# A graph-and-experts kernel on one core: order of TensorE's queue in the first gate, constant products in front of waits, and two starts of loops

## The reference, cut to what matters

```python
x = x + gnn0(layernorm(x), adj)      # U = eigenvectors of the normalised Laplacian (64 x 64);
                                     # U ( relu((U^T x) W1 + b1) W2 + b2 )
x = x + ffn0(layernorm(x))           # 8 experts, top 2 of (x Wg + bg), softmax of the two logits as weights:
                                     # sum_e w_e (gelu(x W1[e] + b1[e]) W2[e] + b2[e]),  hidden size 512
x = x + gnn1(layernorm(x), adj)      # h = relu(adj (x Wg0 + bg0)); h = relu(adj (h Wg1 + bg1));
                                     # then for p = 1..4 an LSTM over windows of p tokens, whose last
                                     # hidden state replaces the last token of its window
x = x + ffn1(layernorm(x))           # H = gelu(x W1 + b1); probs = softmax(H Wg + bg); the expert e of the
                                     # largest prob: prob * (H Wd[e] + bd[e])
```

## Time and profile before

| | |
|---|---|
| time, median of 3 runs | 1427.07 us (1426.35 to 1429.05) |
| the profiled execution's own time | 1429.24 us |
| its span | 1427.5 us |
| TensorE, busy share of the span | 78% (1110.5 us) |
| VectorE | 57% (813.1 us) |
| ScalarE | 52% (747.9 us) |
| GpSimd | 38% (537.7 us) |
| mean granted clock of TensorE | 0.902 |

### The profile page before, as it was taken

The page is one execution under the profiler, slowest core; times in us unless marked ns, Lnnn a source line. Parts: engine busy times, 40 slices in busy tenths (PEclk is TensorE's granted clock), DMA queues, the critical chain, the costliest instruction groups (busy, mean ns, idle before and its releaser), DMA issues. The chain is left out here.

```text
span 1427.5 us, 27849 instructions
## 1 busy us (share of the span) xinstructions
PE 1110.5 (78%) x6302; PEld 823.2 (58%) x6303; DVE 813.1 (57%) x3799; ACT 747.9 (52%) x2079; POOL 537.7 (38%) x837
## 2 busy tenths in 40 slices
PE   3444424568744999999949999999999689929995
PEld 2223313456644999999936663445444245529995
DVE  7777798958772433354558973444444478622221
ACT  4555555515322666666626765655555366415552
POOL 5666513302577770255447500000000005645554
PEclk9999965879757999999969999999999799959998
DMA  9500000000112332333311100000000002243330
GB/s 260 144 1 1 1 1 1 1 4 16 36 64 85 118 120 66 89 103 104 102 46 50 40 1 0 0 1 0 0 1 0 4 6 85 90 130 110 106 103 27
DMA packets 85701, 75.57 MB, mean 53 GB/s; under 512 B 13207, under 2 KB 74848, under 8 KB 85613
## 3 DMA queue, kind: packets, MB, share of 16 engines
q1 hardware_dynamic: 71788, 44.64, 11.3%
q0 software_dynamic: 13824, 29.98, 6.7%
HBM read 41.72 MB, written 33.37 MB: 53 GB/s over the span
## 5 line engine op out<-in xcount | busy, mean ns | idle before, releaser
L1249 POOL DMA_INDIRECT z<-spent,seats x64 | 63.3, 990 | 393.5 <-DVE spent L1370 376.1
L1716 ACT ACTIVATE c_H<-ps,c_b 128x128 f32<-128x128 f32 x576 | 156.9, 383 | 99.5 <-PE ps L1762 99.5
L2278 PE MATMUL ps<-BIG,spent 128*128 x364 | 156.1, 578 | 3.3 <-ACTq L2291 3.3
L1762 PE MATMUL ps<-ZS,c_w 128*128 128x128 f32 x1152 | 142.5, 277 | 2.9 <-ACT ZS L1705 1.7
L1748 PE MATMUL ps<-spent,c_H 128*128 x1152 | 140.3, 275 | 0.0
L1762 PEld LDWEIGHTS ps<-ZS,c_w 128*128 128x128 f32 x1152 | 136.0, 194 | 3.9 <-ACT ZS L1705 2.4
L1748 PEld LDWEIGHTS ps<-spent,c_H 128*128 128x128 f32 x1152 | 134.3, 192 | 0.0
L2278 PEld LDWEIGHTS ps<-BIG,spent 128*128 128x128 f32 x364 | 69.7, 192 | 84.7 <-issue 84.7
L2286 PE MATMUL ps<-e_hs,spent 128*128 128x512 f32 (+1 forms) x256 | 110.0, 572 | 0.0
L897 POOL DMA_INDIRECT z<-BIG,spots x64 | 63.5, 993 | 111.1 <-DVE spots L1014 93.7
L1616 POOL DMA_INDIRECT c_rows<-y,seats x64 | 60.6, 946 | 113.9 <-DMA y<-c_ys 60.0
(11 more groups left out here) (534 smaller groups left out, 2599.2 us busy)
## 6 DMA issues: line engine op xcount, KB each, us to landing
BIG<-z SPq DMA_DIRECT2D x72, 129.0 KB, 2.1
ZB<-z SPq DMA_DIRECT2D x144, 64.0 KB
y<-c_ys SPq DMA_DIRECT2D x72, 128.0 KB
spent<-in_L_ffn_W_dram SPq DMA_DIRECT2D x1, 2048.0 KB
spent<-in_L_ffn_W_dram SPq DMA_DIRECT2D x8, 256.0 KB
w_dn<-in_L_ffn_Wd_dram SPq DMA_DIRECT2D x8, 256.0 KB
z<-BIG,spots POOLq DMA_INDIRECT x128, 2.2
z<-j_padding SPq DMA_DIRECT2D x9, 129.0 KB, 2.6
```

The lines of the kernel that those rows point to most:

```text
L1249: pool.indirect_dma_start(z, bass.IndirectOffsetOnAxis(ap=k.seats[:, 0, n:n + 1], axis=0), k.R[:, row(n), :], None, bounds_check=E * STRID ...
L1716: act.activation(H[u][:, c, h * P:(h + 1) * P], UP[u][c // 2][:, o:o + P], ACT.Gelu, bias=b1[u][h][:, c:c + 1]).then_inc(gelu, 1)
L1762: pe.matmul(UP[u][c // 2][:, o:o + P], w1[u][h][:, c * P:(c + 1) * P], ZT[u][:, h * P:(h + 1) * P], start=True, stop=True).then_inc(up, 1)
L2278: last = pe.matmul(view(k.ps[4 * u + j], wide, lanes), k.w_ihT[:, w, :], state(i, u, s, p, wide, lanes), start=True, stop=(s == 0))
```

## The change

There is a new helper. It issues products of constant bf16 values into a PSUM bank that is free at that place; nothing reads the result.

```diff
 # gate0, VectorE
-            if LAG + 2 <= g <= GROUPS + LAG + 1:
+            if g % 2 and 0 <= g - LAG - 2 < GROUPS:
                 add_gate_bias(g - LAG - 2)
...
             if 2 <= g <= GROUPS + 1:
                 stats(g - 2)
+            if g % 2 and 0 <= g - LAG - 1 < GROUPS:
+                add_gate_bias(g - LAG - 1)
 # gate0, TensorE (mix(g) holds the mixing products that stood at the loop's head)
+        mix(0)
         for g in range(GROUPS + LAG + 4):
...
-            if ranks:
-                rank((g - 11) // 2)
...
-                if ranks:
-                    pe.wait_ge(rank_read, (g - 11) // 2 + 1)
+                if g >= 12:
+                    pe.wait_ge(rank_read, (g - 10) // 2)
...
                 last.then_inc(turned, 1)
+            if g + 1 < GROUPS:
+                mix(g + 1)
+            if ranks:
+                rank((g - 11) // 2)
 # first experts, TensorE (second experts alike)
-            if not known or t < NT - 1:
+            if not known or 0 < t < NT - 1:
                 turn(t + 1, 1 - u, r + u, first)
...
+        pe.wait_ge(k.gate0_scattered, 16 * (TILES - 2))
+        keep_busy(pe, Y[1], k.ones16, 14)
         turn(0, 0, 0, 0)
+        turn(1, 1, 0, 0)
 # gate1, TensorE
+        keep_busy(pe, UP[3], k.ones16, 4)
         for g in range(3):
             lift(g)
+            keep_busy(pe, UP[3], k.ones16, 4 if g < 2 else 12)
...
     def ahead(g):
-        return range(3, LIFTED + 1) if g == 0 else range(g + LIFTED, min(g + LIFTED + 1, GROUPS))
+        return (range(3, 4), range(4, LIFTED + 2))[g] if g < 2 else range(g + LIFTED, min(g + LIFTED + 1, GROUPS))
 # gnn1, VectorE
+            hidden(0)
             for j in range(GT):
                 combine(2 * GT + j)
                 stats(2 * GT + j)
+            add_bias(0)
             for g in range(GROUPS + 2):
-                if 1 <= g <= GROUPS:
+                if 2 <= g <= GROUPS:
                     add_bias(g - 1)
```

More of the change, by code:

```diff
@@ L452, in _ @@
             token_rows(GROUPS - 1)
+            keep_busy(pe, ps[7], both, 5)
             pe.wait_ge(s_vectors, 1)
@@ L455, in _ @@
             pe.wait_ge(s_zw_sb, GROUPS)
+            keep_busy(pe, ps[7], both, 2)
             pe.wait_ge(s_sides, 1)
@@ L464, in _ @@
             pe.matmul(ps[2][0:N, 0:N], U[:, :], LU[:, :], start=True, stop=True).then_inc(s_forms, 1)
+            keep_busy(pe, ps[7], both, 2)
             pe.wait_ge(s_ritz, 1)
             pe.matmul(ps[4][0:N, 0:N], ones[0:N, 0:N], offd[:, :], start=True, stop=True).then_inc(s_ritz_row, 1)
+            keep_busy(pe, ps[7], both, 8)
             pe.wait_ge(s_factor, 1)
@@ L469, in _ @@
             pe.matmul(ps[0][:, 0:N], E2[:, :], UT2[:, 0:N], start=True, stop=True).then_inc(s_refined, 1)
+            keep_busy(pe, ps[7], both, 3)
         @block.vector
@@ L1139, in rank, with mix @@
             pe.matmul(RANK, k.upper16[:, :], marks, start=False, stop=True).then_inc(ranked, 1)
+        def mix(g):
+            if g >= 2:
+                pe.wait_ge(h_ready, g - 1)
+            for j in range(GT):
+                c = slice(j * P, (j + 1) * P)
+                last = pe.matmul(MIX[g % 2][:, c], k.BIG[:, g * GC + j * P:g * GC + (j + 1) * P], k.BDU[:, :],
+                                 start=True, stop=True)
+            last.then_inc(mixed, 1)
+        mix(0)
         for g in range(GROUPS + LAG + 4):
             u = g % 2
[L1143 to L1150, removed]
             if 2 <= g <= GROUPS + 1:
@@ L1402, in gate_vector @@
                 root_of(1, nothing())
-                back(4)
-                back(5)
             elif g % 2 and g + 3 < GROUPS:
+                if g == 1:
+                    back(4)
+                    back(5)
+                    link.need(link.n)
                 spread((g + 3) // 2, beside)
@@ L1529, in gate_tensor @@
             for n in ahead(g):
+                if g == 0:
+                    keep_busy(pe, SC, k.ones16, 4)
                 lift(n)
@@ L1717, in step @@
                                    bias=b1[u][h][:, c:c + 1]).then_inc(gelu, 1)
-            if not (isinstance(t, int) and t == NT - 1):
+            if not (isinstance(t, int) and t in (0, NT - 1)):
                 turn_out(t + 1, 1 - u)
         turn_out(0, 0)
+        turn_out(1, 1)
         for t in range(2):
@@ L1843, in experts_sync @@
         for b in range(RING):
-            sp.wait_ge(k.scattered[b], 16 * PAIR * len(range(b, GROUPS // 2, RING)))
+            sp.wait_ge(k.scattered[b], 16 * sum(n < TILES - 2 for n in range(TILES) if n // PAIR % RING == b))
+        sp.wait_ge(k.last_scattered, 16 * 2)
         def fetch(t, b, r):
@@ L1928, in step @@
             if isinstance(t, int) and t == 0:
+                last = (GROUPS // 2 - 1) % RING
+                pe.wait_ge(k.scattered[last], 16 * (PAIR * len(range(last, GROUPS // 2, RING)) - 2))
+                keep_busy(pe, Y[1], k.ones16, 14)
                 turn(0, 0, 0)
+                turn(1, 1, 0)
             pe.wait_ge(turned_sb, t + 1)
@@ L2192, in _ @@
             pe.matmul(GATE[1][:, 0:D], floor[:, 0:P], k.w_g1[:, 1, :], start=True, stop=True).then_inc(outer, 1)
+            pe.wait_ge(used, GT)
+            keep_busy(pe, GATE[2], k.ones16, 12)
             for g in range(GROUPS + 1):
```

17 lines of the change are left out of this document (11 added, 6 removed).

## The result

The changed kernel takes 1417.12 us (median of 4 runs, 1417.02 to 1419.32), the kernel before 1426.71 in the same comparison (4 runs, 1425.09 to 1429.05): a ratio of 0.9931 with a 95% interval of 0.9919 to 0.9942, some 9.6 us less. The sign is as forecast; the time lies 1.1 us outside the range, and 9.6 of the 22 us came. The two profiled executions took 1429.24 and 1417.02 us, 12.2 apart: that of before lies 2.5 above its median, so 2.6 us of what the two profiles show as gain is not in the medians.

A forecast was written before the change was run, and what follows sets the result against it. TensorE was taken to bound the last stage, VectorE's waits for TensorE the first gate. 2.5 + 10 + 1.9 + 3.8 + 3.0 + 1.0 = 22.2 us turned the 1427.07 median into 1405, range 1400 to 1416 (forecast's own 1400 to 1408).

The forecast's parts named there:

- Price of a product: One constant bf16 product of 512 columns was estimated at 0.43 us at 1.2 GHz and 0.21 us at 2.4.
- End of the spectrum, 2.5: 20 products in waits before the first gate raise the clock for its start: gain 2.5 us, 0 if not risen by 300.
- Ranks last, 10: First gate: the new order removes VectorE's 10.9 us of waits for TensorE, leaving 0.9; gain 10 us (3 to 11).
- 8.7 us a pair: TensorE's work per pair in the first gate's loop at the high clock level, against VectorE's 10.5 us.
- First and second experts, 1.9 and 1.0: Fillers before turn 0, turn 1 before up 0: gains 1.9 us (first experts) and 1.0 us (second, or loss up to 1.0).
- up 0 ... takes 1.8 us instead of 3.6: First experts: up-projection 0 begins later, at 447.1 instead of about 445.6, but takes half as long.
- about 4.8 us before the first turn: First experts: when the 14 products start after scatter 62 landed, so they end 0.2 to 1.0 us late.
- the rival in which the level is lost between fillers and work: Both experts' starts gain nothing (0 and +1.0), the second gate 1.7 us; sum 17.0, time 1410 us; chance 16%.
- Second gate, 3.0: Fillers between lifts speed up 0 to 3.6 us from 5.51; lifts 4 and 5 move behind up 1; gain 3.0 us.
- Second graph stage, 3.8: Hidden 0 and bias 0 move ahead on VectorE, so bias 1 comes at 757.0 instead of 760.80; gain 3.8 us.
- the rival in which the products do no good: Products never raise the level in time: first gate gains 9, graph stage 2.9, others lose 0.6; 1416 us; chance 11%.
- the three signs of being wrong: VectorE's waits reappear under the moved gate bias; level drops in the loop; turn 1's load costs up 0 more than gained.

The follow-up runs named there:

- loop_fill: turn_behind plus 8 constant products in front of the gating products in the first gate's even iterations 8 to 18; 1411.47 us, ratio 0.9892 to the kernel before.
- loop_only: The kernel before with only the first gate's reordering (mixing ahead, ranks last, both gate biases in odd iterations), no constant products; 1420.99 us, ratio 0.9962.
- rank_first: turn_behind with the ranks in front of the next mixing instead of behind it in the first gate's odd iterations; 1409.49 us, ratio 0.9878 to the kernel before.
- pe_order: The kernel before with only TensorE's new order in the first gate; VectorE keeps one gate bias at the start of each iteration; 1431.54 us, ratio 1.0029.
- turn_behind: The changed kernel with turn 1 put back behind up-projection 0 in both experts, fillers kept; 1413.37 us, ratio 0.9910 to the kernel before.
- fill_close: turn_behind with 18 and 20 fillers instead of 14 before turn 0 of the experts, and 2 more before up 0; 1413.83 us, ratio 0.9906.
- late_fill: loop_fill, fill_close and rank_first edits together, more second-gate fillers, and the first gate's loop fillers only from iteration 12; 1406.93 us, ratio 0.9860 to the kernel before.

## Why the prediction missed, step by step

- *Price of a product.* Right: eight take 3.60 us at the low level (0.45 each), and in the loop of `loop_fill` eight take 1.73 us up to their successor at the high one (0.22).
- *End of the spectrum, 2.5.* The step that failed is "at the high level 5.90 us of products would be 2.95": the level was at 0.50 at 300 still, the case for which the prediction itself had put 0. It rose between 303 and 304, in the profile before just ahead of 306; but in `loop_only`, which has no fillers, it rose between 303 and 304 as well. From the first mixing to the first scatter it takes 44.0 us in the changed kernel and 45.2 before, but 43.9 in `loop_only`; and the changed kernel without its products (`no_fill`) has the first scatter at 343.97, against 343.87 with them. These 20 products have shown no gain.
- *Ranks last, 10.* That VectorE needs 10.5 us a pair without its waits was right: three pairs take 31.3 to 31.8 us in the five runs with the loop filled and in `rank_first` (3 x 10.5 = 31.5). The failed step is TensorE's "8.7 us a pair", which I worked out at the high level and took as given. At that level it is right (from the ranks at 340.84 to those at 351.74 it is 10.90 us with a stall of 2.24). But if TensorE has 8.7 us of work in 10.5, it stands for the difference in every pair, and behind the second such stall the clock went down; at the lower level the ranks came late, and VectorE waited. So the order gave 8.2 in the profiled run and less in others: in five profiles with this order and no fillers in the loop, first to last scatter took 85.2 and 85.3 us where the level was 1.00 from 340 to 350, and 88.5, 88.5 and 90.2 us where it was 0.80 to 0.88 there, against 82.3 to 82.5 in the five with the stall filled: the level holds up to 370, and VectorE waits for ranks for 0.6 us at most over three pairs. `rank_first` shows a second part: the ranks stood behind a mixing, and with that mixing behind them VectorE's waits are 0.6 us too. That the moved gate bias would cost nothing was right and too weak, since without it the order loses (`pe_order`).
- *First and second experts, 1.9 and 1.0.* Here most is missing (6.0 of 10 us in the profile). The failed step is "up 0 ... takes 1.8 us instead of 3.6". I had seen that turn 1 makes up 0 wait for its load, and paid for that wait with a fast up 0; behind that wait the clock was low. Up 0 stayed slow and late: `turn_behind` gives 0.6 and 1.9 us back (in the second experts `no_fill` gives 2.2), and in `fill_close` and the four runs with the same fillers, where TensorE hardly stands ahead of it, up 0 is fast. A sum was wrong as well: the start of the 14 products "about 4.8 us before the first turn". The prediction's own rows put scatter 62 at 438.34 - 2 x 1.28 and its landing 2.45 later, 6.2 us ahead of 444.46; so the products were not to end late, but early, and they did, by 1.09 us. This is the rival in which the level is lost between fillers and work, and it was priced too low, since in it I let the new order of the turns cost only 0 and 1.0.
- *Second gate, 3.0.* Half right: 2.2. The failed step is again the fast up 0: it took 5.40 us, hardly less than the 5.51 before, once more behind two stands. The moved lifts did work: up 1 follows 8.1 us behind up 0 instead of 15.0, and up 2 19.9 instead of 22.5.
- *Second graph stage, 3.8.* Right: 3.6 in the profile.

The measured time is that of the rival in which the products do no good (1416), and so are its parts: 9 for the first gate, 2.9 for the graph stage and a loss of 0.6 elsewhere, where the profile has 9.2, 3.6 and a loss of 0.5. `no_fill` bears it out by its median; but that rival's mechanism is not what happened, as the clock did rise in front of both experts and was lost again. Of the three signs of being wrong that the prediction named, two came: the level dropped in the loop, and turn 1's load held up 0 for longer than a faster clock gave back.

On the rule that the prediction weighed ("TensorE: Matmul & The Clock Gate", Part 4, in the Trainium skill: transposes alone do not bring up the fast clock), no run here decides it. The clock was at 1.00 from 433 to 441 in `loop_fill` with nothing but a turn between the fillers and up 0, and what differs between `turn_behind` and `fill_close` is that the stands around the turn are closed. The window of 0.63 that the prediction put down to the rule lies within a stand of 3.50 us, so it cannot tell transposes from standing still either:

```profile
1146.39 1.09 PE L1488 MATMUL ps<-ident,j_S 128*128 128x128 f32 x4 [3.50 <-DVE spent L1271]
```

What stays open: why the clock falls behind some stands and not behind others of the same length; why the same program without fillers spreads over 11 us (its slowest execution has a mean granted clock of 0.903, its fastest 0.910); why the two slow up-projections of the second experts took longer behind fillers that ended early than without any (6.36 against 5.24 us); and whether the spectrum's products do anything.

## What to carry to other kernels

A product that raises the clock is worth nothing if the clock falls again before the work: bring the last one up to the first real product, and fill the short stands behind it too, before counting any gain, and read the granted clock there in more than one profile. When a new order makes another engine the bound, the engine that was relieved begins to stand, and its work is then to be priced at the low clock as well. An instruction moved ahead in a queue brings its own load's wait with it.

## What the runs showed of the hardware

Behind stands of 1.3 to 2.3 us the granted clock went down in some profiles: in the changed kernel's loop from 1.00 (340 to 350) to 0.50 (370 to 380), with stalls of 2.24 and 2.27 us and TensorE otherwise at work, and in front of up 0 of `turn_behind` (1.29 and 0.47 us). Elsewhere it did not: it held behind the first of those two stalls, and in `loop_fill` behind 1.84 and 0.47 us. So the length of a stand alone does not say whether the clock is lost. The fall can show in the stand or only in the work behind it: in the first experts the granted clock is 0.56 within the stand of 1.85 us; in the second gate it is 1.00 up to the end of the stand and falls in the first us of the up-projection, which therefore takes 5.40 us:

```profile
1121.80:1122.50 0.70, 0.03 (x1) 0.00 (x0) 0.70 (x4) 0.63 (x2) 0.00 (x0) 1.00 0.00 0
1122.50:1123.50 1.00, 0.98 (x2) 0.47 (x3) 1.00 (x5) 0.94 (x1) 0.00 (x0) 0.60 0.00 0
```

Whether a kept level makes the times steadier is not shown: runs spread over 11.2 us in `no_fill` and over 2.9 in `late_fill`, but over 2.3 in the changed kernel, whose clock falls too.
